# A decoder on one core: the last two steps of its state-space and cross-attention stage rearranged on TensorE

## The chip, the cores and the metric

The kernel runs on one core of a Trainium2 chip. The time is the device time in microseconds (us) of one execution, given as the median of several. TensorE (PE in the profile) multiplies matrices and writes its results to eight PSUM banks; VectorE (DVE), ScalarE (ACT) and GpSimd (POOL) work on what is there or in SBUF; SyncE (SP) issues transfers. Each engine runs its own list of instructions in order, and they wait for each other through semaphores. TensorE's clock is granted at one of two levels, 1.2 or 2.4 GHz; the profile's PEclk column shows it as 0.50 or 1.00.

## The reference, cut to what matters

The kernel computes a decoder of six blocks over 8 sequences of 256 tokens, width 256, all in float32. The last three are what matters here: a state-space mixer, a cross attention with 8 heads of 64 channels over a context of 256 rows per sequence, and a layer of 8 experts of which each token takes two.

```python
x = x + _L1_attn_ref(_layernorm(x, axis=-1), L1_attn_in_proj_w, ...)      # state-space mixer, out projection 512 -> 256
x = x + _L1_xattn_ref(_layernorm(x, axis=-1), ctx_768, L1_xattn_Wq, ...)  # cross attention
x = x + _L1_ffn_ref(_layernorm(x, axis=-1), L1_ffn_Wr, ...)               # router, top 2 of 8 experts
```

In the cross attention q = norm(x) Wq, k = ctx Wk, v = ctx Wv; per head the weights are softmax(q k / 8), the weighted values are concatenated and go through Wo, and a bias and x are added. The router's logits are norm(x) Wr + br.

## The kernel before, in words

The 2048 tokens are taken as 4 pairs of sequences (`PAIRS`), each of 512 tokens or four tiles of 128 rows. The stage `ssm_and_cross` (line 157) calls `mixer(p, q, n)` on every engine once per step: `n` is the pair whose head (similarity, gates, in projection) runs, `p` the pair in its state-space scan, `q` the pair in its cross attention. The last two steps are (p=3, q=2, n=None), in the following called the last scan step, and (None, 3, None), the lone step, in which only the cross attention of pair 3 is left. The expert layer follows.

In the last scan step PE ends the sums over states for the four channel blocks in banks `pa[0]` to `pa[3]`. DVE multiplies each block by its gate (line 1611 and 1612, semaphore `yg_ready`), and PE does the out projection: it waits for all four blocks and for the last values of pair 3 (`v2_out`), then runs 16 products of 128 rows by 256 columns over the four blocks, into `pa[3]` and `pt[0]` (line 2236). ScalarE's copy of those last values, `last_out(7)`, stands late in its list, behind the copy of the transposed attention rows (line 976). DVE adds the halves to x (1627), takes statistics, adds the last tile of pair 2's cross attention (1536), and normalises the rows of pair 3 (1426). PE transposes these rows (`tail_transposed`), computes the queries in four blocks (`queries`, line 2152), the first scores of the lone step (`scores2(0)`, 2087), transposes the rows for the router (`rows_routed`) and runs the router (2282). DVE adds the router's bias to the logits of pair 2 (1652), and PE waits for that (`logits_ready`, line 2311) before it goes on.

The lone step has 16 units of work, four per tile of 128 queries; a unit holds two heads. For unit u, PE computes the scores (`scores2`, line 2087, 64-row operands) into `pt[1]` or `pt[0]`; DVE takes the maximum over each row, as the minimum of negated scores (1523); ACT takes the exponential (963); PE transposes the weights (`weights_transposed`, 1733); ACT copies them (973); PE multiplies them with the values (`weigh2`, 2115) into one bank, `bank_av` = `po[1]`, that collects a tile. PE's list has, per unit, scores of unit v+1, the weighted values of unit v-1 and the transposes of unit v. After each fourth unit DVE divides (1527 and 1528, semaphore `at2_ready`), PE transposes (1733), ACT copies (976), PE projects with Wo (2201) and DVE adds to x (1536). `weigh2` of a tile's first unit waits for `at2_ready` of the tile before. DVE also does the routing arithmetic of the first twelve tiles between the units (`early_routing`, lines 1322 to 1377), with two small products on PE (`ranks`, into `pa[0]` and `pa[1]`, lines 1964 and 1965). GpSimd sends the rows of these tiles to the experts' buffer meanwhile (663), one tile per unit. After the last tile come normalisation, the router for pair 3, the routing of the last four tiles and the sending of their rows, and then the experts.

Of the kernel before, what the change touches and what calls it, by code (L numbers as in the profile page):

```python
# [13 lines left out]
P = 128  # L14
# [163 lines left out]
class CrossBanks:  # L178
# [3 lines left out]
    def __init__(self, lone, score, tr, out):  # L182
        self.lone, self.score, self.tr, self.rows, self.out = lone, score, tr, out[0], out[1]
# [19 lines left out]
def decoder(nc, t, out):  # L203
# [149 lines left out]
    proj_banks, xp_bank = (pa[3], pt[0]), pa[1]  # L353
    def cross_banks(p, n):

        if p is None and n is None:
            return CrossBanks(True, lone_score, lone_tr, (lone_out, lone_out))
        return CrossBanks(False, (bank_score, bank_score), (bank_tr, bank_tr), (bank_tr, bank_score))
# [374 lines left out]
    def _(act):  # L733
# [92 lines left out]
        def mixer(p, q, n, head_alone=False):  # L826
# [183 lines left out]
            if n is not None:  # L1010
# [5 lines left out]
                conv_silu(0)  # L1016
            if crossing:
                cross(UNITS + 3)
# [28 lines left out]
            if p is not None:  # L1047
                if n is None:
                    last_out(len(LAST_SLOTS) - 1)
# [41 lines left out]
    def _(dve):  # L1091
# [256 lines left out]
        def ranked(first, end, ready):  # L1348
            dve.wait_ge(rank_done, ready)
            total = pa[1][:, 0:NT * NE].rearrange("p (t e) -> p t e", t=NT)  # L1350
# [44 lines left out]
        def mixer(p, q, n, head_alone=False):  # L1395
# [122 lines left out]
            def cross(i):  # L1518
# [5 lines left out]
                if i % 8 == 0 and i >= 8:  # L1524
# [3 lines left out]
                    v.tensor_tensor(at2.rearrange("p (h d) -> p h d", h=QH), bank_av[:, :].rearrange("p (h d) -> p h d", h=QH),  # L1528
# [93 lines left out]
            if p is not None:  # L1622
                rows, pair = rows_of(p), xst[:, ts(p, TT), :]
                for s in range(2):
                    half = xst[:, bass.ds(p * TT + 2 * s, 2), :]
                    dve.wait_ge(proj_done, 2 * p + s + 1)
                    v.tensor_tensor(half, proj_banks[s][:, :].rearrange("p (t d) -> p t d", t=2), half, ALU.add).then_inc(proj_added, 1)
# [22 lines left out]
            if q is not None:  # L1650
                dve.wait_ge(route_done, q + 1)
                v.tensor_tensor(lgall[:, ts(q, TT), :], route_bank[:, 0:TT * NE].rearrange("p (t e) -> p t e", t=TT), wide(r_r, TT), ALU.add)\
                    .then_inc(logits_ready, 1)
# [75 lines left out]
    def _(pe):  # L1729
# [231 lines left out]
        def ranks(first, end, ready):  # L1961
# [3 lines left out]
            mm(pa[1][:, at], ones, flat_sel[:, at], start=True, stop=True).then_inc(rank_done, 1)  # L1965

        def mixer(p, q, n, head_alone=False):
# [111 lines left out]
            def scores2(u, banks=at.score, keys=last_kT if at.lone else kT):  # L2079
# [26 lines left out]
            def weigh2(u):  # L2106
# [4 lines left out]
                if u % 4 == 0 and tile:  # L2111
                    pe.wait_ge(at2_ready, 4 * q + tile)
                for b in range(2):
                    for k in range(2):
                        last = mm(bank_av[:, ts(h0 + 2 * b, QD)], pT[u % 2][:, 2 * b + k, :],
# [314 lines left out]
```

## Time and profile before

| | |
|---|---|
| median of 3 runs | 2406.69 us (2406.55 to 2411.33) |
| profiled execution | 2406.48 us, span 2404.2 us |
| mean granted TensorE clock | 0.918 |
| busy: PE, DVE, ACT, POOL | 2071.9, 1717.4, 1045.5, 333.4 us |
| last scan step's tail, from the last scan to the router's end | 1961 to 2004.8 us |
| lone step, units | 2005.1 to 2092.8 us |
| lone step, last tile to the routing's end | 2092.8 to 2120.7 us |
| first product of the experts | 2142.0 us |

The span goes from the first to the last instruction; the execution's own time is 2.3 us longer. A row of the timeline gives start, length, engine, line, operation, what it writes and reads, the shape and how many instructions are merged in it, and in brackets how long the engine had been idle and who ended that. On TensorE one product of the program shows as two MATMUL records (a transpose as one).

### The profile page before, as it was taken

How to read it: one execution, taken by the hardware profiler on the slowest of the kernel's cores; microseconds unless marked ns; L12 is line 12 of the kernel's file. 1: busy time of each engine (PE TensorE's matmuls, PEld its weight loads, DVE VectorE, ACT ScalarE, POOL GpSimd, SP SyncE). 2: the span in 40 equal slices, each digit the busy share in tenths (PEclk: the TensorE clock that was granted, in tenths of full speed). 3: DMA queues.
4: the chain of work that ended last, by engine and by line, in shares of the span. 5: the costliest groups of instructions: out<-in, count | busy, mean ns of one | idle time of the engine just before them, and what ended most of it. 6: DMA issues, size and time to landing. Idle time of an engine off the chain costs nothing.

```text
span 2404.2 us, 33455 instructions
## 1 busy us (share of the span) xinstructions
PE 2071.9 (86%) x12304; PEld 1272.8 (53%) x12304; DVE 1717.4 (71%) x2514; ACT 1045.5 (43%) x1641; POOL 333.4 (14%) x368
## 2 busy tenths in 40 slices
PE   6999999999999999885659778987798888738998
PEld 4666666666666666542324344444453445525665
DVE  7777777777777778769999999989999983210001
ACT  1222222222222222328675877587758842211221
POOL 1111111111111111100000000000000001352222
PEclk8999999999999999997789888989899996669999
DMA  6000100000000100011111111111111103112442
GB/s 240 1 0 18 31 22 1 18 27 26 1 18 27 32 1 1 1 41 57 53 42 36 42 36 42 37 42 35 35 36 42 53 18 117 42 30 60 115 128 53
DMA packets 62237, 99.77 MB, mean 41 GB/s; under 512 B 13333, under 2 KB 44592, under 8 KB 61585
## 3 DMA queue, kind: packets, MB, share of 16 engines
q1 hardware_dynamic: 55120, 90.10, 11.5%
q0 software_dynamic: 6976, 7.84, 1.7%
q8 instruction: 83, 1.36, 0.2%
q14 instruction: 58, 0.47, 0.1%
HBM read 83.53 MB, written 15.53 MB: 41 GB/s over the span
## 4 chain that ended last, share of the span: by engine, by line
PE 54%; DVE 28%; issue 12%; ACT 4%; DMA 1%; another core or an unknown queue 1%; POOL 0%; DVEq 0%; SPq 0%; ACTq 0%; POOLq 0%
PE po L1806 9%; PE pa L1796 9%; DVE arena L1555 8%; PE pa L1754 4%; PE po L2347 4%; PE pa L2336 4%; DVE arena L1545 4%; PE pt L1771 4%; PE pa L2076 2%; DVE arena L1158 2%; DVE arena L1563 2%; PE pa L1786 2%; DVE arena L1160 1%; PE pa L1845 1%; PE pt L1779 1%
## 5 line engine op out<-in xcount | busy, mean ns | idle before, releaser
L2076 PE MATMUL pa<-arena 128*128 128x512 f32 x512 | 296.4, 708 | 88.2 <-DVE arena L1563 88.2
L1555 DVE TENSOR_TENSOR_SCAN arena<-arena 128x1024 f32<-128x1024 f32 x128 | 292.4, 2284 | 13.3 <-ACT arena L937 13.1
L580 POOL TENSOR_SCALAR arena<-arena 128x2 f32<-128x2 f32 (+1 forms) x92 | 27.2, 296 | 1532.1 <-DVE arena L1420 831.0
L1806 PE MATMUL po<-arena 128*128 128x256 f32 x960 | 224.2, 385 | 0.0
L2076 PEld LDWEIGHTS pa<-arena 128*128 128x128 f32 x512 | 100.2, 215 | 220.2 <-DVE arena L1563 120.0
L1796 PE MATMUL pa<-arena 128*128 128x512 f32 x480 | 212.4, 595 | 4.0 <-ACT arena L754 3.7
L776 ACT COPY arena<-pa 128x512 f32<-128x512 f32 x128 | 65.7, 601 | 323.8 <-PE pa L1754 323.8
L1233 DVE TENSOR_TENSOR arena<-pa,arena 128x512 f32<-128x512 f32 x256 | 158.6, 682 | 62.2 <-PE pa L1754 62.1
L921 ACT ACTIVATE arena<-arena 128x510 f32<-128x510 f32 x256 | 170.5, 717 | 55.1 <-DVE arena L1555 51.9
L1806 PEld LDWEIGHTS po<-arena 128*128 128x128 f32 x960 | 176.8, 189 | 32.8 <-issue 6.0
L1697 DVE TENSOR_TENSOR arena<-po,arena 128x512 f32<-128x512 f32 x14 | 9.7, 692 | 227.0 <-PE po L2347 227.0
L1545 DVE TENSOR_TENSOR arena<-arena 128x1024 f32<-128x1024 f32 x128 | 154.6, 1208 | 7.7 <-PE pa L2076 4.6
L1733 PE MATMUL po<-arena 128*128 128x128 f32 x440 | 78.6, 309 | 92.2 <-ACT arena L963 62.2
L1563 DVE TENSOR_TENSOR arena<-arena 128x1024 f32<-128x1024 f32 x128 | 155.9, 1218 | 0.3
L1796 PEld LDWEIGHTS pa<-arena 128*128 128x128 f32 x480 | 89.8, 189 | 117.2 <-issue 117.0
L932 ACT ACTIVATE arena<-arena 128x1020 int16<-128x1020 f32 x128 | 145.5, 1136 | 1.4 <-ACT arena L921 1.0
L1754 PE MATMUL pa<-arena 32*128 32x128 f32 x3072 | 128.9, 287 | 10.2 <-ACT arena L763 5.5
L937 ACT ACTIVATE arena<-arena 128x1020 f32<-128x1020 int16 x128 | 133.7, 1044 | 0.2
L1754 PEld LDWEIGHTS pa<-arena 32*128 32x128 f32 x3072 | 106.3, 189 | 50.1 <-issue 37.2
L1733 PEld LDWEIGHTS po<-arena 128*128 128x128 f32 x440 | 55.0, 159 | 142.8 <-ACT arena L963 95.4
L763 ACT ACTIVATE arena<-pa,arena 128x512 f32<-128x512 f32 x120 | 82.1, 687 | 98.4 <-PE pa L1796 98.3
L1077 ACT ACTIVATE arena<-pa,arena 128x512 f32<-128x512 f32 x64 | 43.8, 687 | 181.3 <-PE pa L2336 156.9
(255 smaller groups left out, 3779.2 us busy)
## 6 DMA issues: line engine op xcount, KB each, us to landing
arena<-bc_rows SPq DMA_DIRECT2D x64, 512.0 KB, 4.3
arena<-in_L_ffn_W SPq DMA_DIRECT2D x16, 1024.0 KB, 8.7
arena<-in_L_attn_W SPq DMA_DIRECT2D x8, 1024.0 KB, 5.7
rows_to_experts<-arena SPq DMA_DIRECT2D x4, 1024.0 KB, 13.1
arena<-rows_to_experts SPq DMA_DIRECT2D x8, 512.0 KB
out<-arena SPq DMA_DIRECT2D x5, 512.0 KB, 8.9
arena<-in_x SPq DMA_DIRECT2D x4, 512.0 KB, 7.4
arena<-in_rows SPq DMA_DIRECT2D x8, 256.0 KB, 3.2
```

The lines of the kernel that those rows point to most:

```text
L921: last = a_(past_start(dA[i % len(dA)])[:, 2 * n:2 * n + 2, :], dt[:, c, :].rearrange("p (s t) -> p s t", s=2)[:, :, 1:], ACT.Exp, scale=a ...
L932: return step.mark(a_(past_start(steps16[i % 2]), past_start(dA[i % len(dA)]), ACT.Relu, scale=-DECAY_STEPS, bias=const[:, C_MID:C_MID + 1]))
L937: a_(past_start(dA[i % len(dA)]), past_start(steps16[i % 2]), ACT.Copy, scale=-1.0 / DECAY_STEPS, bias=DECAY_TOP).then_inc(da_ready, 1)
L1233: v.tensor_tensor(scm[:, (4 * block + g) % SLOTS, :, :], pa[g][:, :].rearrange("p (h q) -> p h q", h=4), tri.unsqueeze(1).broadcast_to([P, ...
L1545: v.tensor_tensor(uh[i % len(uh)], dtx[:, c, :].unsqueeze(1).broadcast_to([P, NG, W]), Bs[g % 2], ALU.mult).then_inc(u_ready, 1)
L1555: v.tensor_tensor_scan(h.rearrange(flat), decay.rearrange(flat), h.rearrange(flat), 0.0, ALU.mult, ALU.add).then_inc(scan_done, 1)
L1563: v.tensor_tensor(h, h, Cs[g % 2], ALU.mult).then_inc(hc_ready, 1)
L1733: return nc.tensor.transpose(dst, src, ident)
L1754: last = mm(pa[g][:, ts(e, P)], keys, qf[ts(g, 32), c, ts(rows_of, P)], start=True, stop=True)
L1796: last = mm(pa[(i + 2) % 4][:, :], w1[:, k, ts(i, P)], yT[:, k, :], start=k == 0, stop=k == KC - 1)
L1806: last = mm(po[s][:, ts(i, D)], gT[:, c, ts(tile, P)], w2[:, c, :], start=c == 0, stop=c == FM - 1)
L2076: last = mm(pa[c][:, :], ident, uh[i % len(uh)][:, n, :], start=g == 0 and n == 0, stop=g == NS // NG - 1 and n == NG - 1)
```

## The change

Five edits, all in the last two steps.

1. The out projection of the last scan step goes by channel block: PE waits for one block's gate, multiplies it for all four row tiles, and goes to the next. It writes `pa[0]` and `pt[0]`. It stands ahead of the last transposes of pair 2's cross attention, and ScalarE's `last_out(7)` is moved ahead of the copy of these transposes.
2. The weighted values of the lone step alternate between `po[1]` and `pa[1]` by tile, so `weigh2` of a tile waits for the division two tiles before. The `ranks` product that was in `pa[1]` goes to the second part of `pa[0]`.
3. The first scores of the lone step stand ahead of the fourth block of queries.
4. The bias for pair 2's logits is added in the lone step, behind the row maximum of unit 0; PE's wait for it is at the lone step's sub-step 10.
5. `kept_busy(bank, count)` issues `count` products of the identity with 128 rows of keys, 512 columns wide, whose result nobody reads. One stands ahead of the scores of each unit 1 to 15 of the lone step, in the bank that the scores then overwrite; one behind the last weighted values, while DVE divides; six behind the last projection with Wo; seven behind pair 2's last projection with Wo, ahead of the transposes of pair 3; one ahead of the router of the last scan step.

```diff
-    proj_banks, xp_bank = (pa[3], pt[0]), pa[1]
+    proj_banks, last_proj_banks, xp_bank = (pa[3], pt[0]), (pa[0], pt[0]), pa[1]
-            return CrossBanks(True, lone_score, lone_tr, (lone_out, lone_out))
+            return CrossBanks(True, lone_score, lone_tr, (lone_out, lone_out), (bank_av, pa[1]))
...
+            if p is not None and n is None:
+                last_out(len(LAST_SLOTS) - 1)
             if crossing:
                 cross(UNITS + 3)
...
+        def logits_kept(pair):
+            dve.wait_ge(route_done, pair + 1)
+            v.tensor_tensor(lgall[:, ts(pair, TT), :], route_bank[:, 0:TT * NE].rearrange("p (t e) -> p t e", t=TT),
+                            r_r.unsqueeze(1).broadcast_to([P, TT, NE]), ALU.add).then_inc(logits_ready, 1)
         def early_routing(i):
             if i == 0:
+                logits_kept(PAIRS - 2)
                 dve.wait_ge(logits_ready, PAIRS - 1)
                 compared(0, NT - TT)
...
-            mm(pa[1][:, at], ones, flat_sel[:, at], start=True, stop=True).then_inc(rank_done, 1)
+            mm(pa[0][:, NT * NE + first * NE:NT * NE + end * NE], ones, flat_sel[:, at], start=True, stop=True).then_inc(rank_done, 1)
+        def kept_busy(bank, count):
+            for _ in range(count):
+                mm(bank[:, :], ident, last_kT[:, 0, :], start=True, stop=True)
...
+                if at.lone:
+                    kept_busy(banks[u % 2], 1)
                 for b in range(2):
                     last = mm(banks[u % 2][:, b * S:(b + 1) * S], qT[ts(e, QD), 2 * j + b, ts(tile, P)],
...
-                if u % 4 == 0 and tile:
-                    pe.wait_ge(at2_ready, 4 * q + tile)
+                if u % 4 == 0 and tile > ahead:
+                    pe.wait_ge(at2_ready, 4 * q + tile - ahead)
...
+                if at.lone and i == 10:
+                    pe.wait_ge(logits_ready, q)
...
+            if p is not None and n is None:
+                for c in range(IC):
+                    pe.wait_ge(yg_ready, IC * p + c + 1)
+                    if c == 0:
+                        pe.wait_ge(v2_out, TT * p + TT)
+                    for s in range(2):
+                        for i in range(2):
+                            last = mm(last_proj_banks[s][:, ts(i, D)], dtx[:, c, ts(2 * s + i, P)], w_out[:, c, :], start=c == 0 and i == 0, stop=c == IC - 1,
+                                      skip_group_check=True)
+                        if c == IC - 1:
+                            last.then_inc(proj_done, 1)
+            if at.lone:
+                pe.wait_ge(at2_ready, 4 * q + TT - 1)
+                kept_busy(po[1], 1)
             if q is not None:
                 cross(UNITS + 1)
                 cross(UNITS + 2)
...
+            if at.lone:
+                pe.wait_ge(at2_ready, 4 * q + TT)
+                kept_busy(po[1], 6)
+            if p is not None and n is None:
+                pe.wait_ge(late_out, late_base + QC)
+                kept_busy(pa[1], 7)
...
                 for m in range(4):
+                    if n is None and m == 3:
+                        pe.wait_ge(late_out, late_base + LATE - 2)
+                        scores2(0, lone_score, last_kT)
                     queries(m)
...
             if n is None:
                 rows_routed()
+                if p is not None:
+                    kept_busy(pa[1], 1)
                 router(late_base + (LATE if p is not None else 0) + LATE_X)
             if p is not None:
-                if q is not None:
+                if q is not None and n is not None:
                     pe.wait_ge(logits_ready, q + 1)
```

## Rows read from the trace of the kernel before

**Rows 1.** The page's row of the granted clock, 40 slices of 60.1 us.
```profile
PEclk8999999999999999997789888989899996669999
```
**Rows 2.** Busy time by stretch; columns: us, PE, PEld, DVE, ACT, POOL, clock, DMA.
```profile
2005.10:2042.60 37.50, 34.56 (x116) 26.48 (x117) 16.87 (x52) 10.91 (x36) 3.20 (x4) 0.50 0.02 8
2042.70:2052.90 10.20, 7.32 (x41) 5.25 (x40) 3.88 (x7) 4.20 (x15) 4.51 (x5) 1.00 0.18 64
2052.90:2063.10 10.20, 9.85 (x36) 8.41 (x37) 0.00 (x0) 2.28 (x7) 3.38 (x5) 0.50 0.11 39
...
2083.70:2087.00 3.30, 0.93 (x5) 0.47 (x3) 1.02 (x2) 1.27 (x5) 0.53 (x1) 1.00 0.12 40
2087.10:2112.60 25.50, 15.22 (x56) 12.50 (x56) 5.72 (x17) 2.46 (x5) 5.16 (x6) 0.50 0.10 35
```
**Rows 3.** Timeline of PE in the lone step, at both clocks.
```profile
2020.94 1.97 PE L2115 MATMUL po<-arena 128*128 128x64 f32 x8
2022.70 1.06 PE L1733 MATMUL pa<-arena 128*128 128x128 f32 x4
...
2025.70 1.97 PE L2115 MATMUL po<-arena 128*128 128x64 f32 x8
...
2047.94 1.13 PE L2087 MATMUL pt<-arena 64*128 64x256 f32 x4
...
2049.94 0.60 PE L1733 MATMUL po<-arena 128*128 128x128 f32 x4
2050.48 1.13 PE L2087 MATMUL pt<-arena 64*128 64x256 f32 x4
```
**Rows 4.** Timeline of PE and one DVE row, last scan step to unit 0.
```profile
1965.28 1.00 PE L2115 MATMUL po<-arena 128*128 128x64 f32 x8
...
1967.93 0.69 DVE L1612 TENSOR_TENSOR arena<-arena 128x512 f32<-128x512 f32 x1
...
1971.43 5.17 PE L2236 MATMUL pa<-arena 128*128 128x256 f32 x16 [1.25 <-ACT arena L952]
...
1976.43 3.62 PE L2236 MATMUL pt<-arena 128*128 128x256 f32 x16
...
1988.24 1.94 PE L1733 MATMUL po<-arena 128*128 128x128 f32 x8 [6.45 <-DVE arena L1426]
...
1996.42 3.60 PE L2152 MATMUL po<-arena 128*128 128x512 f32 x8
...
2002.83 1.95 PE L2282 MATMUL pa<-arena 128*128 128x8 f32 x16 [0.73 <-ACT arena L906]
...
2010.64 1.97 PE L2115 MATMUL po<-arena 128*128 128x64 f32 x8 [0.49 <-ACT arena L973]
```
**Rows 5.** Timeline of the lone step where one tile ends.
```profile
2032.97 1.97 PE L2115 MATMUL po<-arena 128*128 128x64 f32 x8 [2.45 <-ACT arena L973]
...
2050.14 0.20 DVE L1527 RECIPROCAL arena<-arena 128x8 f32<-128x8 f32 x1 [4.53 <-PE po L2115]
...
2053.25 1.97 PE L2115 MATMUL po<-arena 128*128 128x64 f32 x8 [1.65 <-ACT arena L973]
```
**Rows 6.** Timeline behind a projection with Wo; GpSimd's sending beside it.
```profile
2042.60 0.97 POOL L663 DMA_INDIRECT rows_to_experts<-arena  x1 [0.30 <-issue]
2043.86 0.42 DVE L1536 TENSOR_TENSOR arena<-pa,arena 128x256 f32<-128x256 f32 x1 [11.32 <-issue]
...
2046.46 1.10 PE L2115 MATMUL po<-arena 128*128 128x64 f32 x8 [1.59 <-ACT arena L973]
```
**Rows 7.** Timeline of PE at the lone step's end.
```profile
2095.56 3.78 PE L2201 MATMUL pa<-arena 128*128 128x256 f32 x8 [0.67 <-ACT arena L976]
2106.36 1.94 PE L1733 MATMUL pa<-arena 128*128 128x128 f32 x8 [7.02 <-DVE arena L1426]
2108.97 3.58 PE L2282 MATMUL pa<-arena 128*128 128x8 f32 x16 [0.68 <-ACT arena L906]
```
**Rows 8.** Timeline of ACT among the first expert's products.
```profile
2172.45 0.69 ACT L1077 ACTIVATE arena<-pa,arena 128x512 f32<-128x512 f32 x1 [9.81 <-remote]
```

More of the change, by code:

```diff
@@ L178, with __init__ @@
 class CrossBanks:
-    def __init__(self, lone, score, tr, out):
-        self.lone, self.score, self.tr, self.rows, self.out = lone, score, tr, out[0], out[1]
+    def __init__(self, lone, score, tr, out, av):
+        self.lone, self.score, self.tr, self.rows, self.out, self.av = lone, score, tr, out[0], out[1], av
 class Arena:
@@ L1527, in cross @@
                     step.after(v.reciprocal(sm[:, tile, :], sm[:, tile, :]))
[L1528 removed]
+                    v.tensor_tensor(at2.rearrange("p (h d) -> p h d", h=QH), at.av[tile % 2][:, :].rearrange("p (h d) -> p h d", h=QH),
                                     sm[:, tile, :].unsqueeze(2).broadcast_to([P, QH, QD]), ALU.mult).then_inc(at2_ready, 1)
@@ L1626, in mixer @@
                     dve.wait_ge(proj_done, 2 * p + s + 1)
-                    v.tensor_tensor(half, proj_banks[s][:, :].rearrange("p (t d) -> p t d", t=2), half, ALU.add).then_inc(proj_added, 1)
+                    v.tensor_tensor(half, (proj_banks if n is not None else last_proj_banks)[s][:, :].rearrange("p (t d) -> p t d", t=2), half, ALU.add).then_inc(proj_added, 1)
                 dve.wait_ge(proj_added, 2 * p + 2)
@@ L1649, in mixer @@
                 step_sizes()
-            if q is not None:
-                dve.wait_ge(route_done, q + 1)
-                v.tensor_tensor(lgall[:, ts(q, TT), :], route_bank[:, 0:TT * NE].rearrange("p (t e) -> p t e", t=TT), wide(r_r, TT), ALU.add)\
-                    .then_inc(logits_ready, 1)
+            if q is not None and (n is not None or p is None):
+                logits_kept(q)
             want = (HEAD_STEPS - (HEAD_ALONE if first else 0) if n is not None else 0) + (TAIL_STEPS if p is not None else 0) + (CROSS_STEPS if q is not None else 0)
@@ L2110, in weigh2 @@
                     pe.wait_ge(v2_out, TT * q + 2)
-                if u % 4 == 0 and tile:
-                    pe.wait_ge(at2_ready, 4 * q + tile)
+                if u % 4 == 0 and tile > ahead:
+                    pe.wait_ge(at2_ready, 4 * q + tile - ahead)
                 for b in range(2):
                     for k in range(2):
-                        last = mm(bank_av[:, ts(h0 + 2 * b, QD)], pT[u % 2][:, 2 * b + k, :],
+                        last = mm(at.av[tile % 2][:, ts(h0 + 2 * b, QD)], pT[u % 2][:, 2 * b + k, :],
                                   (last_vv if at.lone else vv)[:, 2 * (tile // 2) + k, ts(h0 + 2 * b, QD)], start=k == 0, stop=k == 1)
@@ L2226, in mixer @@
                 cross(UNITS + 2)
-            if p is not None:
+            if p is not None and n is not None:
                 pe.wait_ge(yg_ready, IC * p + IC)
-                if n is not None:
-                    pe.wait_ge(in_out, 8 * n + 1)
-                else:
-                    pe.wait_ge(v2_out, TT * p + TT)
+                pe.wait_ge(in_out, 8 * n + 1)
                 for s in range(2):
```

10 lines of the change are left out of this document (2 added, 8 removed).

## The prediction

> **What bounds the kernel now.** I first read the page's row of the granted clock [rows 1]: it stands at 7 to 9 nearly everywhere and at 6 in three slices next to each other, 1984 to 2164 us: queries, router, lone step, and the sending of rows behind it. Then busy time by stretch [rows 2]. From 2005.1 to 2042.6 us TensorE is busy 34.56 of 37.5 us, and the clock is 0.50 (1.2 GHz) throughout; DVE has 16.87 us and ACT 10.91. So the lone step is bound by TensorE at half its clock, not by VectorE as the scans are. From 2042.7 the clock alternates: 10.2 us at 1.00 with PE busy 7.32 of them, 10.2 us at 0.50 with PE busy 9.85, the same pair again (not shown), 3.3 us at 1.00, and from 2087 to the last router 0.50. What did the engine do before each rise? At 2042.6, 2063.1 and 2083.6 it had just spent 1.4 to 1.8 us in the projection with Wo, 128 rows by 256 columns. Before the falls it had an idle gap (1.65 us before 2053.25 [rows 5]) or a run of small products (the router's 8 columns, before 2005 [rows 4]).
>
> Then the timeline, for the price of a unit at both clocks [rows 3]. At 0.50, weighted values start at 2020.94 and at 2025.70: 4.76 us a unit. At 1.00, scores start at 2047.94 and 2050.48: 2.54 us. These are full-rate loops of PE, with no wait in them. Last I followed the waits where a unit isn't PE-bound, in rows 5 and 6.
>
> **Edit 5, the unread products.** A product of 512 columns shows as two records. The last two query blocks are four such products, eight records in 3.60 us, which is 7 starts of 0.43 and an end of 0.59 [rows 4]: 0.86 us a product at clock 1.00. At 0.50 I take twice that, 1.7 us (an estimate by the ratio of the two clocks). Thus a dense unit becomes 2.54 + 0.86 = 3.40 us if the clock stays at 1.00, against 4.76 now: a gain of 1.36. If it stays at 0.50, the unit costs 6.5 us: a loss of 1.7. Everything hangs on the clock. For the rise speaks that a full-array product of 1.4 us sufficed three times, and that the new one, at low clock, is 1.7 us of the widest form in every unit. For staying up speaks that PE's gaps are filled with part of it. I take the high clock for nearly all of the step.
>
> **Edit 2, the second bank, I cost at nothing.** PE's first weighted values of a tile wait 1.65 us for ACT's copy L973, not for the bank [rows 5]. ACT's list has that copy behind the exponential of the next unit, that waits for DVE's maximum, and this stands behind the division in DVE's list. So the copy always comes after the bank is free. The price of a tile's end stays: from DVE's reciprocal at 2050.14 (previous values just done) to 2053.25, 3.1 us. In it PE does 0.5 of transposes and 1.1 of scores; the new product fits in the gap. Where DVE also has the placing of twelve tiles to do, the same is 2027.70 to 2032.97, 5.3 us. Bounds of edit 2: 0 to a gain of 1 us.
>
> **Edit 1, projection by channel block.** Now 16 products, two records each, run from 1971.43 to 1976.43 + 3.62 = 1980.05, partly at the low clock [rows 4]. In the new order they begin behind the last weighted values, 1965.28 + 1.00 = 1966.3; the first three gates are done before PE comes to them, and the fourth at 1967.93 + 0.69 = 1968.62. The last values of pair 3 are copied ahead of that. PE has no gap from 1963 on, so I take the high clock: 32 records at 3.62/16 = 0.226 are 7.0 us with start-up, end 1973.3. DVE's addition, now at 1980.1, comes 6.75 us sooner, and so do the rows for PE's transposes: 1988.24 becomes 1981.5. Behind the projection PE still has 0.7 of transposes, ACT's copy and a Wo projection (1.9), until about 1976.7. Then come seven products, 6.0 us, until 1982.7. They overrun the rows by 1.2 us; that is edit 5's price here. Their return is the clock: eight transposes at about 1.1 instead of 1.94 us, and eight query products at 6.9 instead of 9.0.
>
> Edit 3 moves 1.1 us of scores past nothing that is late: the router waits for all queries anyway, 0 to 0.5. From the start of transposes to that of the router is 14.6 us now [rows 4]; new: 1.1 + 0.75 for the copy + 6.9 + 1.1 scores + 1.1 transposes + 0.9 for the unread product, which covers the copies = 11.85. The router starts at 1982.75 + 11.85 = 1994.6 instead of 2002.83: 8.2 sooner.
>
> Edit 4: the maximum of unit 0 no longer waits for the router, but unit 1's still has the three comparisons of about 0.95 us ahead of it, that need the logits. From router start to first weighted values (2010.64) is 7.8 us; I take 7.4. Gain so far 8.6 us.
>
> **The lone step, summed.** Units 0 to 3 go from 2010.64 to 2027.7, 17.0 us; new three units of 3.40, small rank products 0.6, last values 1.1: 11.9. Gain 5.1, so 13.7. Tile 0 to tile 1: now 2027.7 to 2050.14, 22.4. New, all at 1.00: 5.3 (tile end) + 1.1 values + 1.0 for eight transposes + 1.9 scores with product + 1.05 values + 0.5 transposes + 1.9 projection + 2.6 for the chain behind it (2043.86 to 2046.46 [rows 6]; the unread product hides there) + 1.05 + 0.5 + 1.9 + 1.1 = 19.9. Gain 2.5, so 16.2. The next tile is the same with 3.1 for 5.3: 17.7 against 20.4 (2050.14 to 2070.52, the same row of the next tile). Gain 2.7, so 18.9. The last tile, 2070.5 to the end of the last Wo projection at 2095.56 + 3.78 = 2099.34 [rows 7], is 28.8 now; new 14.3 up to unit 14's values, then transposes 0.5, copy 0.6, values 1.1, division 0.95 (the single unread product beside it), transposes 0.6, copy 0.6, projection 1.9: 20.5. Gain 8.3, so 27.2. Behind it 7.0 us of DVE and POOL remain, with six unread products of 5.2 inside. Then transposes 1.1 for 1.94 and router 2.0 for 3.58 [rows 7]: gain 2.4. Sum 29.6 us with the clock at 1.00 everywhere.
>
> GpSimd doesn't bound this: it sends a tile's row pair in 2 x 1.27 us, twelve pairs in 31 us [rows 6], and has some 47 us from unit 4 to unit 15. Everything behind the router moves rigidly.
>
> The clock won't be high everywhere. Two gaps remain that are as long as those before which it fell: 2.9 us in the first tile's end, and 2.6 behind the third Wo projection (that one from 2084.6 to 2087.3 ended at 0.50 [rows 2]). The dense part behind a gap is 7.5 us at 1.00 and 12.4 at 0.50, so a fall costs up to 4.9; since unread products now stand in it, I take 3 us for one of the two. 29.6 - 3 = 26.6. On the profiled execution, 2406.48, that is 2379.9; it stands 0.2 below the median of the runs, so 2380.
>
> Here the Trainium skill has a rule against me: TensorE: Matmul & The Clock Gate, Part 4 (PE-mode transpose), says that in a kernel's context full rate doesn't engage for transposes. But four transposes took 1.06 us at clock 0.50 and 0.60 at 1.00 [rows 3], so this trace disagrees, and it decides. By the rule the sum would be some 6 us smaller, for 13 groups of four in the dense parts.
>
> **Rivals.**
> (a) The clock alternates in the lone step as now, because a product per unit is too little at the tile ends. For it: it did fall with PE busy 7.32 of 10.2 us. Against: up to 1.7 us of that idle time is now filled. The first 13.7 us hold, but each later tile has a dense part of 12.4 instead of 10.7, some at 0.50, and loses about 2.3: 13.7 - 7 + 1 = 8 gained, 2399.
> (b) The other side: the unread products don't lift the clock among scores of 64 rows and narrow values. Place: the 37.5 us at 0.50 [rows 2], in which PE was 92% busy and no rise came. Price: 1.7 us in each dense unit. 8.6 is gained up to unit 0; units 0 to 3 lose 5.2, the three tiles 2.4 each, the six products at 1.7 overrun the 7.0 us gap by 3.3, and the 10 us stretches now at 1.00 may go to 0.50, some 5. Net 12 slower, 2418. It decides once the mean clock of the step stays below about 0.65.
> (c) It goes better: both gaps are bridged, and ACT's stalls among the first expert's products, three long ones such as 9.81 us [rows 8] that no engine shown here releases, get shorter. 2373 or less. They may as well get longer: I allow 3 us either way.
> (d) The change doesn't do what it says: the products are hidden and the clock stays as it was, gain of edits 1, 3 and 4 given back: 2405.
>
> **Chances.** Forecast 0.70, (a) 0.14, (b) 0.04, (c) 0.08, (d) 0.04. The forecast's own range is 2374 to 2387; with most of (a) it is 2373 to 2398. About 0.2%, 4.8 us, is what a measurement tells from no change. Faster 0.92, same 0.04, slower 0.04.
>
> **What would show it.** Projection done at about 1973 and the transposes of line 1733 begun at 1982 to 1983, clock 1.00 there. Router start near 1994.6. Units 3.4 us apart, clock 1.00 in most of 1997 to 2080. Waits of the first weighted values of a tile still on ACT's copy, none on the bank. The last router 30 us sooner than 2108.97. I am wrong if the units are over 4.8 us apart, or if the clock falls in each tile, or if the time from the last router to the end changes by more than 3 us.

## The result, and the profile after

| | before | changed |
|---|---|---|
| median | 2409.01 us (2406.55 to 2420.47, 4 runs) | 2382.2 us (2380.23 to 2387.01, 4 runs) |
| profiled execution | 2406.48, span 2404.2 | 2387.01, span 2384.8 |
| mean granted clock | 0.918 | 0.933 |

The ratio over the runs is 0.9873, 95% interval 0.9844 to 0.9903 (the quotient of the two medians is 0.9889, inside it): 27 us faster by the medians. The profiled execution of the changed kernel is the slowest of its four; 19.4 us lie between the two profiled ones. The clock's row of the page, answer to [rows 1], has one slice at 6 where three stood side by side:

```profile
PEclk8999999999999999997789987989899999969999
```

Busy time by stretch of the changed kernel, answer to [rows 2]; the columns are the same (us, PE, PEld, DVE, ACT, POOL, clock, DMA):

```profile
2003.00:2020.60 17.60, 14.10 (x77) 9.44 (x77) 12.00 (x46) 6.59 (x23) 0.00 (x0) 1.00 0.01 1
2021.00:2024.50 3.50, 3.50 (x16) 3.13 (x16) 0.00 (x0) 1.31 (x5) 1.20 (x1) 0.52 0.00 0
2024.60:2068.50 43.90, 38.11 (x206) 26.57 (x204) 8.83 (x16) 15.31 (x51) 18.53 (x19) 1.00 0.16 59
2068.60:2078.90 10.30, 9.15 (x24) 6.34 (x25) 1.56 (x4) 1.00 (x2) 3.90 (x4) 0.51 0.10 35
2079.00:2089.00 10.00, 7.79 (x36) 4.49 (x34) 4.08 (x14) 1.07 (x2) 1.28 (x2) 1.00 0.16 53
```

The lone step, at 0.50 for 37.5 us without a break before, runs at 1.00 but for 3.5 and 10.3 us. The two falls stand behind its two largest gaps (2.94 and 2.65 us below). The timeline of PE, answer to [rows 4], then a dense unit (L1973 is the unread product), the first two tile ends, and the end:

```profile
1968.23 1.08 PE L2243 MATMUL pa<-arena 128*128 128x256 f32 x4
...
1974.34 1.02 PE L2243 MATMUL pt<-arena 128*128 128x256 f32 x4
...
1978.31 6.17 PE L1973 MATMUL pa<-arena 128*128 128x512 f32 x14
1984.32 1.04 PE L1737 MATMUL po<-arena 128*128 128x128 f32 x8
...
1996.20 1.95 PE L2311 MATMUL pa<-arena 128*128 128x8 f32 x16
...
2003.55 1.10 PE L2125 MATMUL po<-arena 128*128 128x64 f32 x8 [0.87 <-ACT arena L973]
2004.49 0.61 PE L1737 MATMUL pa<-arena 128*128 128x128 f32 x4
2004.94 1.02 PE L1973 MATMUL pt<-arena 128*128 128x512 f32 x2
2005.89 1.13 PE L2097 MATMUL pt<-arena 64*128 64x256 f32 x4
2006.95 1.10 PE L2125 MATMUL po<-arena 128*128 128x64 f32 x8
...
2020.60 1.70 PE L2125 MATMUL pa<-arena 128*128 128x64 f32 x8 [2.94 <-ACT arena L973]
...
2039.66 1.10 PE L2125 MATMUL po<-arena 128*128 128x64 f32 x8 [0.79 <-ACT arena L973]
...
2066.84 1.10 PE L2125 MATMUL pa<-arena 128*128 128x64 f32 x8 [2.65 <-ACT arena L973]
...
2074.38 3.78 PE L2213 MATMUL pa<-arena 128*128 128x256 f32 x8 [0.68 <-ACT arena L976]
...
2086.97 1.95 PE L2311 MATMUL pa<-arena 128*128 128x8 f32 x16 [0.73 <-ACT arena L906]
```

Weighted values of two dense units start 3.40 us apart (2003.55, 2006.95); they were 4.76 apart at 0.50. The waits at tile ends name ACT's copy. The last router runs at high clock, 1.95 us against 3.58.

Behind the router, one row differs most from the prediction's rigid shift: ACT among the first expert's products (answer to [rows 8]) in the changed kernel. Three of its activations start 10.5 us apart, of which it is idle 9.8:

```profile
2124.90 0.69 ACT L1077 ACTIVATE arena<-pa,arena 128x512 f32<-128x512 f32 x1 [3.81 <-PE pa L2367]
2135.39 0.69 ACT L1077 ACTIVATE arena<-pa,arena 128x512 f32<-128x512 f32 x1 [9.80 <-issue]
2145.89 0.69 ACT L1077 ACTIVATE arena<-pa,arena 128x512 f32<-128x512 f32 x1 [9.81 <-remote]
2153.60 2.42 ACT L1077 ACTIVATE arena<-pa,arena 128x512 f32<-128x512 f32 x4 [7.02 <-remote]
```

To compare runs I count from the end of pair 2's last weighted values (1966.28 before, 1968.39 changed) in the profiled executions. "Ranks end" is the end of the last small rank product, "experts begin" the start of the first transposes of the expert layer. That zero point lies between 1964.9 and 1975.8 us in the fourteen profiles, so up to 11 us of difference arise ahead of the changed stage.

| run | router start | unit 0's values | unit 3 ends | unit 7 ends | last Wo ends | ranks end | experts begin |
|---|---|---|---|---|---|---|---|
| before | 36.6 | 44.4 | 61.4 | 83.8 | 133.1 | 150.0 | 173.0 |
| changed | 27.8 | 35.2 | 46.9 | 68.1 | 109.8 | 124.3 | 148.8 |
| changed, again | 27.8 | 35.2 | 46.9 | 72.9 | 115.6 | 130.1 | 154.3 |
| e1 no products | 29.9 | 37.2 | 54.3 | 80.0 | 126.4 | 143.3 | 166.2 |
| e2 products alone | 35.0 | 45.1 | 56.8 | 79.4 | 122.3 | 136.8 | 161.1 |
| e3 no unit products | 27.8 | 35.2 | 52.2 | 77.7 | 127.0 | 141.5 | 164.9 |
| e4 unit products only | 29.9 | 39.5 | 51.3 | 73.8 | 116.2 | 133.2 | 156.0 |
| e5 one bank | 27.8 | 35.2 | 46.9 | 68.1 | 109.8 | 124.3 | 148.4 |
| e6 old projection | 35.1 | 42.4 | 54.2 | 76.4 | 115.8 | 130.3 | 153.0 |
| e7 transposes | 27.8 | 35.2 | 46.9 | 68.2 | 109.8 | 124.3 | 148.8 |
| e8 gaps filled | 27.1 | 34.4 | 46.1 | 67.4 | 105.4 | 119.9 | 144.6 |
| e9 gaps alone | 27.1 | 34.4 | 50.5 | 69.0 | 105.7 | 121.8 | 146.1 |
| e10 early and gaps | 27.1 | 34.4 | 46.2 | 64.7 | 101.4 | 117.5 | 141.6 |
| e11 tags early | 27.1 | 34.4 | 47.8 | 66.3 | 108.1 | 123.9 | 147.2 |

The times of one kernel spread by a little over 1%: on the chip of e1 to e4, 23 runs of the kernel before lay between 2398.74 and 2426.21, with mean clocks of 0.910 to 0.920. The profiled one, 2406.48 at 0.918, is on the fast side. So a stage from one profile is exact for that execution only, and a difference of 5 us between kernels needs both the stage and the times.

### The profile page after: what moved, and what is told of

Its sections match the earlier page's. It is cut to its first block, busy times and chain, and to the rows that moved or that the text cites. A ratio compares the mean times of both kernels' runs of the same rounds, so it can differ in the third digit from the quotient of the medians.

```text
span 2384.8 us, 33574 instructions
## 1 busy us (share of the span) xinstructions
PE 2072.3 (87%) x12364; PEld 1260.1 (53%) x12364; DVE 1717.6 (72%) x2514; ACT 1045.8 (44%) x1641; POOL 334.0 (14%) x368
## 4 chain that ended last, share of the span: by engine, by line
PE 53%; DVE 28%; issue 10%; ACT 4%; DMA 2%; another core or an unknown queue 1%; POOL 0%; DVEq 0%; SPq 0%; ACTq 0%; POOLq 0%
PE po L1810 9%; PE pa L1800 9%; DVE arena L1561 8%; PE pa L1758 4%; PE po L2378 4%; DVE arena L1551 4%; PE pt L1775 3%; PE pa L2084 3%; PE pa L2367 3%; DVE arena L1158 2%; DVE arena L1569 2%; DMA arena<-rows_to_experts 2%; PE pa L1790 1%; DVE arena L1160 1%; PE pt L1783 1%
## 5 line engine op out<-in xcount | busy, mean ns | idle before, releaser
L2084 PE MATMUL pa<-arena 128*128 128x512 f32 x512 | 297.9, 711 | 85.8 <-DVE arena L1569 85.8
L1561 DVE TENSOR_TENSOR_SCAN arena<-arena 128x1024 f32<-128x1024 f32 x128 | 292.5, 2285 | 13.5 <-ACT arena L937 13.3
L1800 PE MATMUL pa<-arena 128*128 128x512 f32 x480 | 212.5, 595 | 4.4 <-ACT arena L754 4.1
L1810 PEld LDWEIGHTS po<-arena 128*128 128x128 f32 x960 | 176.8, 189 | 32.9 <-issue 6.0
L1569 DVE TENSOR_TENSOR arena<-arena 128x1024 f32<-128x1024 f32 x128 | 156.0, 1219 | 0.3
L1737 PE MATMUL po<-arena 128*128 128x128 f32 x440 | 74.6, 297 | 83.0 <-ACT arena L963 62.3
L2367 PE MATMUL pa<-arena 128*128 128x512 f32 x256 | 119.0, 622 | 17.1 <-ACT arena L1077 10.6
```

The lines of the kernel that those rows point to most:

```text
L1561: v.tensor_tensor_scan(h.rearrange(flat), decay.rearrange(flat), h.rearrange(flat), 0.0, ALU.mult, ALU.add).then_inc(scan_done, 1)
L1569: v.tensor_tensor(h, h, Cs[g % 2], ALU.mult).then_inc(hc_ready, 1)
L1800: last = mm(pa[(i + 2) % 4][:, :], w1[:, k, ts(i, P)], yT[:, k, :], start=k == 0, stop=k == KC - 1)
L1810: last = mm(po[s][:, ts(i, D)], gT[:, c, ts(tile, P)], w2[:, c, :], start=c == 0, stop=c == FM - 1)
L2084: last = mm(pa[c][:, :], ident, uh[i % len(uh)][:, n, :], start=g == 0 and n == 0, stop=g == NS // NG - 1 and n == NG - 1)
L2367: last = mm(pa[m % 4][:, :], w1e[j][:, c, ts(m, P)], xgT[:, c, :], start=c == 0, stop=c == KC - 1)
```

## The experiments

**e1, without any unread product.**
```diff
-                if at.lone:
-                    kept_busy(banks[u % 2], 1)
...
-                kept_busy(po[1], 1)
...
-                kept_busy(po[1], 6)
...
-                kept_busy(pa[1], 7)
...
-                    kept_busy(pa[1], 1)
```


> The changed kernel without any unread product; projection by block, second bank, first scores ahead and the moved logits stay. Measure: from the end of pair 2's last weighted values to the last small rank product, 148.9 us before and 123.2 us in the changed kernel. Theory T, the high clock brings two thirds of the gain and only the projection (6.75 us) and the freed row maximum (0.4 us) are left: 141 to 142 us, time near 2401, clock 0.50 from the queries' start and in most of the lone step. Rival R1, the new order alone brings the gain and the clock follows from it: under 132 us, near 2390. Rival R2, the second bank lets the units run on: tile ends under 2 us instead of 3.1, stage 136 us.

Median 2400.61 against 2418.35, ratio 0.9933 (0.991 to 0.9957). Ranks end at 143.3. The long stretch of low clock is back; e1:

```profile
1996.70:2034.40 37.70, 34.60 (x117) 26.50 (x117) 16.65 (x52) 9.89 (x32) 3.48 (x4) 0.50 0.02 8
```
By the stage T nearly holds (1.3 us above its range): without products 6.7 us of 25.7 are left. R1 (under 132) and R2 (136) are out. By the times half of the gain is left (0.67% of 1.27%), more than T says; with intervals of 0.25 to 0.3% to either side and a kernel before whose slower runs also have the lower mean clocks, the split by time stays rough.

**e2, only the products, on the kernel before.**
```diff
+                if at.lone:
+                    kept_busy(banks[u % 2], 1)
...
+            if at.lone:
+                pe.wait_ge(at2_ready, 4 * q + TT - 1)
+                kept_busy(po[0], 1)
...
+                kept_busy(po[0], 6)
...
+                kept_busy(pa[1], 7)
...
+                    kept_busy(pa[1], 1)
```


> The kernel before with only the unread products added (same places and counts; those behind the tiles go to bank po[0], which is free there with one bank of weighted values). T: all of the clock's part of the gain, without the projection's 6.75 us, but the seven products no longer overrun the rows by 2.1 us, so stage 148.9 - 25.7 + 6.75 - 1.5 = 128 to 129 us, time near 2388. R1: products without the new order cost their own time, 150 us or more, no gain. R2: since weighted values of a tile's first unit wait for the division, tile ends of 3.1 us grow by 0.9 and four of them cost 3 to 4 us: 132 us.

2391.69 against 2418.35, ratio 0.9894 (0.9863 to 0.9925), ranks end 136.8: a clear gain, so R1 is out, but 8 us short of T in the stage. R2 is out too: the first tile's end has the same wait, 2.94 us. The units' part is as in the changed kernel (unit 0's values to the last Wo product: 77.2 us against 74.6); what lacks is in front. PE still waits here for pair 2's logits (edit 4 isn't in this run), and the clock falls during the first product behind that wait; e2:

```profile
2004.08 1.95 PE L2297 MATMUL pa<-arena 128*128 128x8 f32 x16
2006.32 1.64 PE L1969 MATMUL pt<-arena 128*128 128x512 f32 x2 [0.28 <-DVE arena L1652]
2007.88 2.07 PE L2093 MATMUL pt<-arena 64*128 64x256 f32 x4
```
From router start to unit 0's values are 10.1 us here, 7.35 in the changed kernel and 7.8 before: at low clock a product ahead of the scores lengthens that path. By these profiles the order edits and the products bring 6.7 and 13.2 us alone and 25.7 together. That they help each other isn't shown by it: a second profile of the changed kernel (below) has 19.9, the plain sum, and by the times the parts are 0.67% and 1.06%, together 1.27%.

**e3, without the 15 products in the units**, and **e4, with only these.**
```diff
 # e3
-                if at.lone:
-                    kept_busy(banks[u % 2], 1)
 # e4
-                kept_busy(po[1], 1)
...
-                kept_busy(po[1], 6)
...
-                kept_busy(pa[1], 7)
...
-                    kept_busy(pa[1], 1)
```


> The changed kernel without the 15 products ahead of the scores; the 7, 1, 1 and 6 others stay. T, the products in the units hold the clock among scores and narrow values: router start is 8 us sooner as in the changed kernel, then the clock falls by the first tile's end at the latest and the lone step alternates as before; stage 134 to 138 us, time near 2395. Rival R3, the clock once high stays high through the dense units by itself and the 15 products cost 0.86 us each where PE is dense: stage 118 to 121 us, time near 2379.

> The changed kernel with only the 15 products ahead of the scores. T: queries and first units as slow as before (router start only 6.5 to 7 us sooner), the units' products lift the clock within the first units; router of pair 3 at 0.50. Stage 126 to 128 us, time near 2386. Rival (b) of the prediction, the products don't lift a low clock among scores and narrow values: units of 6.5 us, stage over 150 us.

e3: 2401.16, ratio 0.9945 (0.9916 to 0.9973), ranks end 141.5. The router is as early as in the changed kernel, then the clock falls and stays; e3:

```profile
1999.60:2036.90 37.30, 32.41 (x111) 24.88 (x109) 14.46 (x50) 9.90 (x32) 4.17 (x4) 0.50 0.04 15
```
R3 is out, and T's 134 to 138 was too good: the stage is only 1.8 us shorter than in e1, and the times are the same (2401.16 and 2400.61). e4: 2390.71, ratio 0.9895 (0.9849 to 0.9941), ranks end 133.2 where T said 126 to 128. Units 0 to 3 take 11.7 us from the first values, as in the changed kernel, so rival (b) of the prediction is out: the clock was low behind the router and rose among the first units, where it stayed low for 37.7 us without any product (e1); e4:

```profile
1999.90:2006.50 6.60, 6.60 (x15) 3.27 (x14) 5.19 (x7) 1.50 (x5) 0.00 (x0) 0.51 0.01 2
2006.70:2023.50 16.80, 14.40 (x78) 9.44 (x76) 10.94 (x44) 5.60 (x21) 0.00 (x0) 1.00 0.00 0
```
The units' products thus help TensorE to its high level and keep it there. But router start to unit 0 is 9.6 us, and the end behind the last Wo product 16.9 us against 14.5. The 15 products outside the units are worth 8.9 us in the stage beside the changed kernel's first profile, 3.0 beside its second.

**The changed kernel again.**

> The changed kernel once more, on the same chip and beside the same runs of the kernel before as the next three. From the end of pair 2's last weighted values to the last small rank product (ranks_end): 150.0 us before and 124.3 in its first profile. Both theories: 122 to 128; the spread shows how much the moment at which the clock changes moves from run to run.

2388.23 against 2415.88, ratio 0.9871 (0.9837 to 0.9904): the result repeats. Its profile has ranks end at 130.1, outside my 122 to 128: all rows up to unit 3 agree within 0.05 us, and the clock falls at the same place behind the first tile's gap, but stays low for 13.6 us instead of 3.5, and for 14 instead of 10 at the end. The same code, 6 us apart, by the clock alone. In the 13.3 us shown TensorE was never idle, had an unread product and the projection with Wo in it, and no rise came before their end; changed, again:

```profile
2028.20:2041.50 13.30, 13.30 (x43) 10.24 (x44) 0.00 (x0) 1.98 (x6) 4.17 (x4) 0.50 0.12 41
```

**e7, transposes in place of the units' products.**
```diff
-                    kept_busy(banks[u % 2], 1)
+                    for _ in range(2):
+                        for k in range(4):
+                            transposed(banks[u % 2][:, ts(k, P)], last_kT[:, 0, ts(k, P)])
```


> The changed kernel with eight transposes of 128x128 in place of each of the 15 products ahead of the scores (the other 15 products stay). Eight transposes took 1.04 us at the high clock and 1.94 at the low one, about as long as a product. T as I now hold it, it is the wide product that lifts and holds the clock, not the filled time: clock falls behind the router as without unit products and ranks_end is at 155 us or more, slower than before. Rival R4, what counts is that TensorE has no gap: ranks_end 123 to 127, like the changed kernel.

2380.46, ratio 0.9846 (0.9814 to 0.9879); ranks end 124.3, and no column of the table is 0.1 us from the changed kernel's. My theory that the wide product does it falls; R4's number comes out, though e9 below shows that having no gap isn't enough. e7 by stretch, and PE behind the first tile's gap:

```profile
1996.10:2018.60 22.50, 18.77 (x130) 15.27 (x129) 16.66 (x52) 7.55 (x26) 0.00 (x0) 1.00 0.03 9
2018.70:2022.50 3.80, 3.80 (x20) 3.80 (x21) 0.00 (x0) 1.26 (x4) 1.15 (x1) 0.55 0.00 0
2022.60:2066.90 44.30, 38.32 (x258) 31.66 (x256) 8.82 (x16) 15.62 (x51) 18.54 (x20) 1.00 0.17 58
```
```profile
2018.69 1.66 PE L2127 MATMUL pa<-arena 128*128 128x64 f32 x8 [2.93 <-ACT arena L973]
2020.14 1.91 PE L1737 MATMUL pa<-arena 128*128 128x128 f32 x8
2021.84 1.35 PE L1737 MATMUL pt<-arena 128*128 128x128 f32 x8
```
Here the clock rose behind narrow values and among sixteen transposes, no wide product among them.

**e8, the three largest gaps filled too.**
```diff
+                if at.lone and i == 30:
+                    pe.wait_ge(pexp_ready, 16 * q + 15)
+                    kept_busy(at.score[0], 2)
+                if at.lone and i == 32:
+                    pe.wait_ge(pexp_ready, 16 * q + 16)
+                    kept_busy(at.score[1], 1)
...
-                    kept_busy(banks[u % 2], 1)
+                    kept_busy(banks[u % 2], 3 if u == 6 else 1)
...
-                kept_busy(pa[1], 7)
+                kept_busy(pa[1], 6)
```


> The changed kernel with unread products also in its three largest gaps: three instead of one ahead of unit 6's scores (gap 2.94 us), two ahead of unit 14's weighted values (2.65), one ahead of unit 15's; and six instead of seven ahead of pair 3's transposes. T: the two falls (2021.0 to 2024.5 and 2068.5 to 2078.9) go, ranks_end 118 to 119.5 us, time 5 us under the changed kernel. Rival R5, the gaps are not what lets it fall (or the added products delay what they precede): 124 to 127.

2380.82, ratio 0.9851 (0.9815 to 0.9886). The time is 7.4 us under that of the changed kernel on the same chip (2388.23), the intervals overlap. Ranks end 119.9, 0.4 above the range. The fall at the end is gone (unit 7 to last Wo 38.0 us against 41.7). The first tile's fall is not: the products cut the wait from 2.94 to 1.23 us, and the clock fell at the same place for the same 3.4 us, so T is wrong there; e8:

```profile
2024.92 1.70 PE L2125 MATMUL pa<-arena 128*128 128x64 f32 x8 [1.23 <-ACT arena L973]
```
```profile
2025.20:2028.60 3.40, 3.40 (x17) 3.26 (x17) 0.00 (x0) 1.09 (x4) 0.97 (x1) 0.51 0.00 0
```
Over all profiles the gaps do count. In the seven with the units' products and both gaps open (changed twice, e2, e4, e5, e6, e7) the clock fell in or just behind both of them; in the four with both filled (e8 to e11) it fell there in e8 alone, behind the first (e9 and e11 have falls elsewhere).

**e9, products only in gaps and the first two units**, and **e10, with those of units 3 to 5 back.** Both keep e8's edits; the lines are against e8's condition.
```diff
-                if at.lone:
+                if at.lone and (u < 3 or u in (6, 8, 10, 12, 14)):   # e9
+                if at.lone and (u < 7 or u in (8, 10, 12, 14)):      # e10
```


> As e8, but without the products of units 3, 4, 5, 7, 9, 11, 13 and 15, where TensorE has no wait that hides them. T' (once high, the dense units hold the clock by themselves, the products matter only in gaps): ranks_end 113 to 116 us. Rival R6 (scores of 64 rows and narrow values don't hold it, seen without unit products as the fall behind the router): falls within units 2 to 5, ranks_end 122 to 132.

> As e9, with the products of units 3, 4 and 5 back: products ahead of units 1 to 6, 8, 10, 12 and 14 and in the gaps; none in units 7, 9, 11, 13 and 15, which held the high clock in e9 without one. If T' holds: units 0 to 3 as in e8 (46.1 instead of 50.5 at the end of unit 3), the rest as in e9: ranks_end 114 to 117, time near 2376, 2 to 5 us under e8 and e9. If the clock's level is a matter of when it happens to be looked at: 118 to 124.

e9: 2379.99, ratio 0.9845 (0.981 to 0.9879). e9 by stretch:

```profile
2002.50:2019.40 16.90, 16.90 (x60) 13.04 (x60) 7.65 (x33) 4.82 (x16) 0.00 (x0) 0.50 0.00 1
2019.60:2080.90 61.30, 52.79 (x269) 35.66 (x267) 17.32 (x43) 19.69 (x61) 24.93 (x26) 1.00 0.14 49
```
Ranks end 121.8, between the two ranges; T' and R6 hold in part. The clock fell behind unit 0's values and did not rise for 16.9 us, although TensorE was busy in every one of them; it rose with unit 6's three products, and then units 7, 9, 11, 13 and 15 kept it for 61.3 us without one. But the fall isn't due to the missing products: it begins before the first place where one is left out, the scores at 2003.36, and in e11, which has all the early ones, it comes at the same place and lasts 3.4 us; e9, then e11:

```profile
2002.49 0.94 PE L1737 MATMUL pa<-arena 128*128 128x128 f32 x4
2003.36 2.07 PE L2097 MATMUL pt<-arena 64*128 64x256 f32 x4
```
```profile
2001.40:2004.80 3.40, 3.40 (x9) 1.80 (x9) 2.48 (x12) 1.50 (x5) 0.00 (x0) 0.50 0.00 0
```
What the products of units 3 to 5 can have done is to end the low stretch sooner, and with the changed kernel's 13.6 us in mind one execution of each doesn't prove that. e10 joins the good parts:

```profile
1996.30:2079.00 82.70, 71.98 (x373) 48.71 (x372) 31.20 (x84) 26.96 (x87) 24.88 (x26) 1.00 0.15 52
```
No fall between router and last Wo product, ranks end 117.5 (0.5 above the expected 114 to 117), 2376.77 against 2410.84, ratio 0.9844 (0.9815 to 0.9873). That this kernel is better than e8 is a matter of 2.4 us in one profile each; the ratios (0.9844, 0.9851) don't tell them apart. In e9 and e10 the last router is back at 0.50 (3.58 us).

**e5, one bank for the weighted values.**
```diff
-            return CrossBanks(True, lone_score, lone_tr, (lone_out, lone_out), (bank_av, pa[1]))
+            return CrossBanks(True, lone_score, lone_tr, (lone_out, lone_out), (bank_av, bank_av))
...
-                if u % 4 == 0 and tile > ahead:
-                    pe.wait_ge(at2_ready, 4 * q + tile - ahead)
+                if u % 4 == 0 and tile:
+                    pe.wait_ge(at2_ready, 4 * q + tile)
...
-                kept_busy(po[1], 1)
+                kept_busy(po[0], 1)
...
-                kept_busy(po[1], 6)
+                kept_busy(po[0], 6)
```


> The changed kernel with one bank for the weighted values and the old wait for the division, everything else kept (the unread products behind the tiles go to po[0]). The prediction's step: the bank is never what comes last, since ACT's copy stands behind DVE's division anyway: tile ends 3.1 us as in the changed kernel, ranks_end 124 to 130, time the same within 3 us. Rival: the second bank frees 1 us or more per tile end, ranks_end 3 to 4 us later than the changed kernel's at the same clock.

2385.87, ratio 0.9888 (0.9853 to 0.9922); the interval overlaps the changed kernel's. Up to ranks end the stage agrees to 0.02 us with the changed kernel's first profile, and so do the first two tile-end waits; e5:

```profile
2022.76 1.68 PE L2125 MATMUL po<-arena 128*128 128x64 f32 x8 [2.94 <-ACT arena L973]
...
2041.82 1.10 PE L2125 MATMUL po<-arena 128*128 128x64 f32 x8 [0.79 <-ACT arena L973]
```
The second bank is worth nothing, as predicted: with one bank the wait still ends with ACT's copy.

**e6, the old projection.**
```diff
-            if p is not None and n is None:
-                last_out(len(LAST_SLOTS) - 1)
...
+                if n is None:
+                    last_out(len(LAST_SLOTS) - 1)
...
-            if p is not None and n is None:
-                for c in range(IC):
-                    pe.wait_ge(yg_ready, IC * p + c + 1)
...
-            if p is not None and n is not None:
+            if p is not None:
                 pe.wait_ge(yg_ready, IC * p + IC)
+                if n is not None:
+                    pe.wait_ge(in_out, 8 * n + 1)
+                else:
+                    pe.wait_ge(v2_out, TT * p + TT)
```


> The changed kernel with the projection as before (all blocks awaited, banks pa[3] and pt[0], last values copied late), everything else kept. The prediction's step prices it at 6.75 us, of which the seven products' overrun (here gone) gives 1.2 to 2 back: router start 33 to 34 us after pair 2's last weighted values instead of 27.8, ranks_end 129 to 131. Rival, from e2 (14 us less than it should): without the projection the clock falls before the queries and the units begin low; ranks_end 133 to 138.

2390.7, ratio 0.9904 (0.9875 to 0.9932). Router start 35.1, 7.3 us later than changed and above the 33 to 34 expected; ranks end 130.3, 6.0 later, in the range. e6:

```profile
1976.94 6.29 PE L2251 MATMUL pa<-arena 128*128 128x256 f32 x16 [1.25 <-ACT arena L952]
1983.07 3.63 PE L2251 MATMUL pt<-arena 128*128 128x256 f32 x16
```
The block order saves the old one's waits and 2.6 us of a projection partly at low clock (9.8 us against 7.1). The clock did not stay low into the units (units 0 to 3 take 11.7 us), so the rival is out.

**e11, e10 with slot tags sent earlier.**
```diff
+                if places == 1 and i % 2:
+                    send_tags(i // 2, i // 2 + 1, 1)
...
                 if p is None:
                     pool.sem_inc(xf_kept, 1)
+                    send_tags((NT - TT) // 2, NT - TT - 1, 1)
...
+        send_tags(NT - TT - 1, NT, 2)
```


> As e10, and GpSimd sends 22 of its 32 pairs of slot tags earlier: tiles 0 to 5 between the row pairs of the lone step, 6 to 10 in the wait for the last routing. Then 10 instead of 32 follow the rows. Theory: ACT's stalls among the first expert's products (28 us here, 23 before the change) last as long as GpSimd issues tags, 41 us; with 13 us of them the stalls shrink to some 8 us and the time falls by 12 to 20 us, to near 2360. Rival: the stalls are code loading of ACT's and stay: same time as e10. Second risk: the earlier tags delay rows and the last normalisation, up to 5 us.

2364.76 against 2410.84, ratio 0.9802 (0.9772 to 0.9832), the best version, 12 us under e10 where I expected 12 to 20. ACT has no stall left in the first expert, where I expected some 8 us; e11:

```profile
2119.70 0.69 ACT L1083 ACTIVATE arena<-pa,arena 128x512 f32<-128x512 f32 x1 [2.63 <-PE pa L2379]
2122.09 0.69 ACT L1083 ACTIVATE arena<-pa,arena 128x512 f32<-128x512 f32 x1 [1.70 <-PE pa L2379]
2123.81 0.69 ACT L1083 ACTIVATE arena<-pa,arena 128x512 f32<-128x512 f32 x1 [1.03 <-PE pa L2379]
```
From the experts' first transposes to the end are 245.9 us, against 263.9 in e10 and 261 to 268 in all other runs. In each of the 13 profiles with late tags ACT's last stalled activation starts 4.0 to 6.2 us behind the start of the last tag send, wherever that is (2153.60 behind 2147.43 in the changed kernel). So the stalls end with the stream, and the rival, code loading, is out. The lone step pays some of it: 6.4 us to ranks end, more than the 5 expected. Part of it is a clock that fell twice, once behind a new wait of 2.67 us at the fourth tile: DVE begins the division ahead of it at 2051.13, though the values were done at 2049.21.

## Why the prediction was right

The time, 2380 against 2382.2, and most steps came out, counted from the same point as in the table. The mechanism is shown too: without the products the clock stays low and 6.7 of the 25.7 us are left (e1).

- **Projection.** Predicted 7.0 us long and done 7.0 us after the last values: 1968.39 to 1975.36, 6.97. (My working, 32 times 0.226, gives 7.2, not 7.0; the projection took 7.1 and its first record starts 0.16 before the last values end.) The overrun of the seven products, predicted 1.2 us: they end at 1984.5, DVE's rows at 1983.4, 1.1. Router start predicted 28.3, measured 27.8. The edit, priced at 6.75, is worth 6.7 without any product (e1 against before, with edit 3) and 7.3 with them (e6), the overrun already paid.
- **Logits and first scores.** Predicted 7.4 us from router to unit 0's values, measured 7.35.
- **Units.** 3.40 us, as summed. Unit 3 ends at 46.9 (predicted 47.6), unit 7 at 68.1 (67.5), unit 11 at 85.5 (85.2).
- **Second bank at nothing.** Right, with its mechanism: e5.
- **The mis-sized term is the last tile.** "Gain 8.3": from unit 11's end to the last Wo product's are 24.2 us instead of the 20.5 summed, against 28.8 before, so 4.6. PE waited 2.65 us, the clock fell at 2068.6, and the last Wo product took 3.78 us as before. The allowance, 3 us for one of two gaps, was meant for this; both gaps had a fall, 1.6 and 3.7 us. Ranks end was 25.7 sooner; I had 26.6 with the allowance. With the gap filled (e8) there is no fall and the same stretch takes 20.6 us, as summed, and e9 to e11 have no fall there either.
- **"Everything behind the router moves rigidly"** was wrong by more than the 3 us I allowed in this execution: 4.2 us from the router's end to the end of the span (295.9 against 291.7), 2.6 from its start, since the router itself is 1.6 shorter. From ranks end to the experts' transposes 1.6 us more, and from there to the end 2.7 more (267.6 against 264.9), in ACT's stalls. Over all runs with late tags this last stretch varies from 261.0 to 267.6, and the changed kernel's second profile has 263.9, so it is no effect of the change that could be shown. A further 2.1 us of the profiled execution lies ahead of the stage, before the changed code. 25.7 - 1.6 - 2.7 - 2.1 = 19.3, the difference of the two profiled spans (19.4).
- **What was luck.** I counted from one profiled execution, 2406.48, with a median of 2406.69 beside it. On the three other occasions the kernel before had medians of 2410.84 to 2418.35, and the changed kernel once more had 2388.23, outside my 2374 to 2387. In the stage its two profiles save 25.7 and 19.9 us, of which only the first meets the 26.6. What repeats is the ratio, 0.9873 and 0.9871; mine was 0.9889.
- **Rivals.** (a) didn't come: two falls, not one per tile, though "changed, again" shows how near it is. (b) is refuted by e4 and the changed kernel. (c) didn't come: neither gap was bridged, and ACT's stalls got longer. e8, e10 and e11 show that both parts of it can be had by other edits. Rival (d), the clock as it was, is refuted by the stretches.
- **My reason for the clock was too narrow.** I argued from 128-row products of 256 columns before each rise, and credited the wide form. e7 shows that eight transposes per unit do the same. The Trainium skill's TensorE: Matmul & The Clock Gate, Part 4 (PE-mode transpose), says of transposes in one kernel's context that full rate doesn't engage, and that they don't count as busy the same way. The trace disagrees twice, in the duration (0.61 us for four at 1.00, 1.06 at 0.50) and in e7.

What stays open: what makes the clock fall and rise where it does. Units without a product stay low for 37.7 us (e1), but it isn't idle time alone: e9 had 16.9 us at 0.50 without a gap, and the changed kernel 13.3 us with a product in it. It isn't the dense mix alone, since the same mix held 1.00 for 61.3 us in e9 itself. In e7's rise the two operations just before were of 128 rows; in the low stretches scores with 64-row operands alternate with them. A run with the scores' operands on all 128 rows would tell; it wasn't made. That the 64 rows matter is a guess, and the changed kernel's long low stretch had 128-row products in it as well. Open too is how much of the 27 us each edit brings in time, beyond e1 to e6's intervals.

## What to carry to other kernels

Read the granted clock beside TensorE's busy share: a stage that is 92% busy at 0.50 has time to give even if no work leaves it (a dense unit went from 4.76 to 3.40 us here with a product added), and work that nobody reads can buy it, most of all in gaps where it delays nothing. Put it into the gaps and where the level must first be reached. Whether to take it out of dense units once the level is held stays open: it was kept without them in e9 and e10, for 2.4 us in one profile (e10 against e8) and nothing that the times show. A second buffer brings nothing where another engine's list already orders the release before the next use, as in e5: check what the wait's last releaser is. And take more than one profile of a kernel whose clock is near a change.

## What the runs showed that I had not expected

- The same code can differ by 6 us in one stage through the moment at which the clock rises again, with everything up to the fall equal to 0.05 us.
- GpSimd's stream of 8-byte-per-row indirect sends, one every 1.28 us, goes with stalls of ACT: activations start up to 10.5 us apart, and 1.72 us apart when most of these sends were earlier (e11). ACT doesn't touch what is sent. The cause isn't shown: a path that both use is a guess, and the row sends at a lower rate in the lone step went with no such stalls.
- Eight transposes of 128x128 take 1.04 us and one product of 512 columns 1.02 us at the high clock, and they replace each other without a trace in the stage (e7).
